# Mamba layer and gated FFN on one core: the dt products of two channel blocks in the upper and the lower rows of the array, with new order lists for the steady and the first chunk

## The chip, the core and the metric

The kernel runs on one core of a Trainium2 chip. That core has five engines that work side by side, each through its own list of instructions in order: TensorE (PE, matmuls, with its weight loads shown apart as PEld), VectorE (DVE), ScalarE (ACT), GpSimd (POOL) and SyncE (SP, which here only issues DMAs). They wait for one another through semaphores. The metric is the device time of one execution in microseconds. Before the change it is 1844.32 us, the median of 3 runs (1843.4 to 1846.78).

## The reference, cut to what matters

The input x is 8 rows of 1024 tokens of 256 channels, all float32. One layer is a Mamba block and a gated FFN, each with a residual and a LayerNorm. The part that the change touches is the step from `dbl` to `dt`.

```python
xz = einsum('bld,ed->ble', x, W_in); xi, z = split(xz, 2)           # 512 + 512 channels
u = silu(causal_conv4(xi, conv_w) + conv_b)
dbl = einsum('blc,ec->ble', u, W_xproj)                             # 16 + 16 + 16 columns
dt = softplus(einsum('blr,cr->blc', dbl[..., :16], W_dt) + b_dt)    # the dt products: K = 16
Bs, Cs = dbl[..., 16:32], dbl[..., 32:48];  A = -exp(A_log)         # 16 states
h = h * exp(dt_t * A) + (dt_t * u_t) * B_t;   y_t = sum_s h * C_t   # a scan over the tokens
y = (y + u * D_skip) * silu(z);  x1 = layernorm(x + y @ W_out.T)
out = layernorm(x1 + (silu(x1 @ wg.T) * (x1 @ wu.T)) @ wd.T)        # 768 hidden channels
```

## The kernel before

**Tiling.** The tokens are worked on in 16 chunks of 512, two for each of the 8 rows (`half` 0 and 1, the second going on from the state of the first). The 512 inner channels are 4 blocks (`cb`) of 128 partitions. A chunk has 64 scan steps, one for each block and state. A step is an `exp` on ACT (`decay_step`, into one of three PSUM banks), half a `drive` product on POOL (two states each, four buffers), and a scan on DVE (`scan`). Four steps make a quad, of which there are 16. PE transposes each quad's states (`transposes`, 4 groups g per quad), ACT copies each group to SBUF (`hT`, `evacuate`), and PE multiplies them with diagonals of C and sums over the states (`sum_states`, into the bank `yb`). Those products are 32 columns wide and the four of a group stand in the four column strips of the array.

**Stages.** Three chunks are in work at once. While the scans of chunk k run, the head of chunk k+1 (products `xi`, convolution, `u`, `xproj`, `dt`) and the tail of chunk k-1 (`out`, LayerNorm, `x1T`, `gate`, `up`, `down`) are put between them. All dense products share a ring of two PSUM banks in a fixed order (`products_in_order`, `room`), so each waits until the product two places before it is evacuated. The first chunk has no tail, and the last no head.

**Order.** Tables of numbers set which side item follows which scan step on each engine: a key (q, j) is a place after step j of quad q, and -1 is ahead of the quad's first. There are tables for steady chunks (`PE_SIDE`, `ACT_SIDE`, `DVE_SIDE`, `POOL_SIDE`), for the first (`..._FIRST`) and for the last (`..._LAST`). At the same place the engines are at different steps: ACT at step 4q+2+j, DVE at 4q+j, PE transposes the quad before, POOL makes drive 2q+j.

**The dt products.** `copy_dbl` (ACT) writes the 48 rows of `dbl`. `dt_proj` (PE) then multiplies the zero-padded `w_dt` (128 rows, of which 16 hold numbers) with `dbl` for each of the four blocks: a full-array product with 512 columns, which the profile shows as two MATMUL records. `add_bias` (ACT), `clamp` (DVE), `softplus_log` (ACT), `softplus_max` (DVE) and `dt_times_u` (POOL) follow. SP sends `dbl`'s B and C rows to DRAM and back, B spread over all partitions (`spread_bc`, `load_b`).

**POOL and the convolution.** `heads` on POOL prepares the first columns of `xi` for a later chunk and waits until all 12 taps of `conv` are done on DVE. All drives behind it wait with it.

**Setup.** Ahead of the first chunk each engine runs the head of chunk 0. There DVE makes `dtu` of block 0 alone (semaphore `f_dtu`), which is all that the first drives need; POOL makes that of block 1 itself in `drive_unit`.

## Time and profile before

| what | value |
|---|---|
| median of 3 runs | 1844.32 us |
| profiled execution: its own time | 1845.17 us |
| profiled execution: its span | 1843.2 us |
| PE busy | 1752.4 us (95%) |
| ACT busy | 1697.6 us (92%) |
| DVE busy | 1675.2 us (91%) |
| POOL busy | 1494.4 us (81%) |
| DMA queue q1, share of 16 engines | 18.3% |
| chain that ended last, by engine | PE 52%, ACT 25%, DVE 10%, issue 9%, POOL 3% |

The span is from the first to the last instruction, and 2.0 us of the execution's time lie around it. Busy shares are means over the whole span. What a stage is worth is read from a stretch of it. A PE busy time is a union of pipelined matmuls, whose ends are modelled.

### The profile page before, as it was taken

Reading aid. Unit: us, or ns where it says so; the run is one execution under the profiler, and the core shown is the slowest. Engines: PE = TensorE matmul, PEld = TensorE weight load, DVE = VectorE, ACT = ScalarE, POOL = GpSimd, SP = SyncE. Lnnn points to the kernel's source line nnn. Section 1 sums busy time; section 2 is a strip of 40 time slices with the busy share of each in tenths; the row PEclk is TensorE's granted clock in tenths of the full one; section 3 lists DMA queues with packets and bytes.
Section 4 is the critical chain, followed back from the end, with each engine's and each line's share of the span. In section 5 each row is a group of like instructions: output and inputs, shape, how many; then the busy total and the mean of one; then the engine's idle time right before and its main releaser. Section 6 shows DMA issues by size and latency. Waiting matters only on the chain.

```text
span 1843.2 us, 40373 instructions
## 1 busy us (share of the span) xinstructions
PE 1752.4 (95%) x15674; PEld 1213.6 (66%) x15674; DVE 1675.2 (91%) x1946; ACT 1697.6 (92%) x2927; POOL 1494.4 (81%) x847
## 2 busy tenths in 40 slices
PE   6679999999999999999999999999999999999997
PEld 2446676766667676676766667676676766667676
DVE  4999999999989999899989999999998999989984
ACT  5899999999999999999999999999999999999981
POOL 1997997879888787987879788787997879798950
PEclk9899999999999999999999999999999999999999
DMA  7030121301313120131301213130131311112000
GB/s 205 2 98 21 4 115 15 115 14 4 125 4 115 15 93 35 3 116 15 115 15 26 102 3 116 15 115 13 4 115 15 115 15 54 74 4 104 24 2 23
DMA packets 171342, 100.56 MB, mean 55 GB/s; under 512 B 139392, under 2 KB 157568, under 8 KB 162960
## 3 DMA queue, kind: packets, MB, share of 16 engines
q1 hardware_dynamic: 171152, 97.98, 18.3%
q8 instruction: 124, 2.03, 0.5%
q14 instruction: 66, 0.54, 0.1%
HBM read 88.52 MB, written 9.44 MB: 53 GB/s over the span
## 4 chain that ended last, share of the span: by engine, by line
PE 52%; ACT 25%; DVE 10%; issue 9%; POOL 3%; ACTq 0%; POOLq 0%; DVEq 0%
PE ring L1132 21%; PE tp L1111 15%; PE yb L1125 8%; ACT hT L684 7%; ACT decay L677 7%; DVE h L882 6%; PE ring L1220 4%; POOL drive L549 2%; ACT xi L695 1%; ACT sz L700 1%; ACT res L743 1%; ACT acc L693 1%; ACT u L710 1%; DVE acc L903 1%; ACT sz L714 1%
## 5 line engine op out<-in xcount | busy, mean ns | idle before, releaser
L549 POOL TENSOR_TENSOR drive<-dtu,b_all 128x1024 f32<-128x1024 f32 x512 | 1212.5, 2397 | 45.4 <-DVE h L882 41.2
L677 ACT ACTIVATE decay<-dt,a_neg 128x512 f32<-128x512 f32 x1024 | 702.7, 711 | 25.8 <-DVE h L882 24.7
L1111 PEld LDWEIGHTS tp<-ident,h 128*128 128x128 f32 x4096 | 462.0, 141 | 273.6 <-issue 153.1
L1111 PE MATMUL tp<-ident,h 128*128 128x128 f32 x4096 | 578.4, 278 | 64.8 <-ACT hT L684 47.9
L684 ACT ACTIVATE hT<-tp 128x512 f32<-128x512 f32 x1024 | 591.4, 606 | 46.8 <-PE tp L1111 44.9
L882 DVE TENSOR_TENSOR_SCAN h<-decay,h,drive 128x512 f32<-128x512 f32 x512 | 622.5, 1270 | 11.8 <-ACT decay L677 11.6
L882 DVE TENSOR_TENSOR_SCAN h<-decay,drive 128x512 f32<-128x512 f32 x512 | 592.9, 1210 | 23.1 <-ACT decay L677 21.3
L1125 PE MATMUL yb<-hT,diag_c 128*32 128x128 f32 x8192 | 273.9, 276 | 0.0
L1125 PEld LDWEIGHTS yb<-hT,diag_c 128*32 128x32 f32 x8192 | 209.9, 110 | 67.5 <-issue 44.4
L1132 PE MATMUL ring<-xt,w_in 128*128 128x512 f32 x512 | 238.3, 600 | 6.4 <-ACT xi L695 3.8
L903 DVE SCALAR_TENSOR_TENSOR acc<-xi,cw,acc 128x512 f32<-128x512 f32 x192 | 155.6, 830 | 29.4 <-ACT xi L695 25.4
L1132 PE MATMUL ring<-xt,w_u 128*128 128x512 f32 x360 | 169.5, 593 | 0.0
L1132 PE MATMUL ring<-xt,w_g 128*128 128x512 f32 x360 | 168.1, 596 | 0.0
L1132 PEld LDWEIGHTS ring<-xt,w_in 128*128 128x128 f32 x512 | 91.1, 192 | 88.9 <-issue 82.4
L568 POOL TENSOR_TENSOR spare_g<-eps,minus 128x4 f32<-128x4 f32 x17 | 4.1, 240 | 159.6 <-DVE acc L903 159.5
L579 POOL TENSOR_TENSOR dtu<-dt,u 128x1024 f32<-128x1024 f32 x31 | 74.1, 2390 | 58.3 <-DVE dt L917 58.3
L1220 PE MATMUL ring<-w_d,xi 128*128 128x256 f32 x480 | 113.5, 379 | 0.0
L1196 PE MATMUL ring<-w_out,yg 128*128 128x256 f32 x480 | 110.1, 382 | 0.1
L1132 PEld LDWEIGHTS ring<-xt,w_g 128*128 128x128 f32 x360 | 62.4, 190 | 59.8 <-issue 49.7
L1196 PEld LDWEIGHTS ring<-w_out,yg 128*128 128x128 f32 x480 | 88.8, 190 | 13.9 <-issue 3.1
L563 POOL TENSOR_TENSOR yg<-yg,sz 128x512 f32<-128x512 f32 x63 | 87.4, 1387 | 11.9 <-DVE yg L893 7.7
L1220 PEld LDWEIGHTS ring<-w_d,xi 128*128 128x128 f32 x480 | 88.9, 190 | 11.0 <-DVE hid L942 0.2
(128 smaller groups left out, 1612.2 us busy)
## 6 DMA issues: line engine op xcount, KB each, us to landing
...
c_col<-bc_scratch SPq DMA_DIRECT2D x256, 2.0 KB, 2.5
...
w_g<-in_w_gT SPq DMA_DIRECT2D x1, 768.0 KB, 7.1
w_u<-in_w_uT SPq DMA_DIRECT2D x1, 768.0 KB, 7.5
```

The costliest lines, as they stand in the source:

```text
L549: tt(drive[:, j % 4, :, :], src, b_all[:, n:n + 2, :], ALU.mult).then_inc(g_dr, 1)
L563: tt(yg[:, cb, :], yg[:, cb, :], sz[:, cb, :], ALU.mult).then_inc(g_y, 1)
L579: tt(dtu[:, two, :], dt[:, two, :], u[:, k.parity, two, :], ALU.mult).then_inc(g_dtu, 1)
L677: act(decay[decay_slot(k.parity, i)][:, :], dt[:, cb, :], ACT.Exp, scale=a_neg[:, cb, n:n + 1]).then_inc(a_da, 1)
L684: act(hT[:, (64 * k.index + g) % HTS, :], tp[g % 2][:, :], ACT.Copy).then_inc(a_ev, 1)
L882: nc.vector.tensor_tensor_scan(h[:, h_slot(k.parity, q), at:at + T, i % 4], decay[decay_slot(k.parity, i)][:, :], drive[:, (i // 2) % 4, i ...
L903: stt(acc[:, cb, :], xi[:, cb, tap:tap + T], cw[:, cb, tap:tap + 1], acc[:, cb, :], ALU.mult, ALU.add).then_inc(v_conv, 1)
L1111: last = nc.tensor.transpose(tp[g % 2][:, b * P:(b + 1) * P], h[:, h_slot(k.parity, q), t0:t0 + TS, :].rearrange("p t s -> p (t s)"), iden ...
L1125: last = mm(yb[b * TS:(b + 1) * TS, f * P:(f + 1) * P], diag_c[:, q % 4, 4 * f + b, :], hT[:, (64 * k.index + g) % HTS, b * P:(b + 1) * P] ...
L1132: last = mm(bank, lhsT, rhs, start=i == 0, stop=i == len(pairs) - 1)
L1196: last = mm(bank(k, "out", i)[:, half * DM:(half + 1) * DM], yg[:, c, tb * P:(tb + 1) * P], w_out[:, c, :], start=c == 0, stop=c == CB - 1)
L1220: last = mm(bank(k, "down", i)[:, half * DM:(half + 1) * DM], hidden_block(m)[:, tb * P:(tb + 1) * P], w_d[:, m, :], start=m == 0, stop=m ...
```

## The change

Three things are changed.

- `w_dt` gets a second copy of its 16 rows at partition 64, by one more DMA of the setup. In each chunk but the first SP also copies `dbl`'s 16 dt rows from partition 0 to partition 64, ahead of the copy to DRAM (semaphore `st_two`).
- For chunks 1 to 15 the dt products of two blocks are issued together as `dt_pair`: block cb from rows 0 to 63 of the array, block cb+1 from rows 64 to 127, into the two ring banks. Chunk 0 keeps the four single products.
- The eight tables of the steady and the first chunk are new. Those of the last chunk are as they were.

```diff
 PE_SIDE = {
-    (3, 3): [("xi", 2), ("xi", 3)], (4, 1): [("out", 0)], (4, 2): [("sum", 2), ("out", 1)],
-    (4, 3): [("xproj", 0)], (5, 2): [("sum", 3), ("dt", 0)], (5, 3): [("x1T", 0)],
+    (2, 3): [("sum", 0)], (3, 1): [("out", 0)], (3, 3): [("out", 1)], (4, 0): [("sum", 1)],
+    (4, 1): [("xproj", 0)], (4, 2): [("sum", 2)], (5, 0): [("dt", 0), ("dt", 1), ("sum", 3)],
...
 DVE_SIDE = {
-    (4, 1): [("max", 1), ("conv", 0, 1), ("conv", 1, 0), ("conv", 1, 1), ("conv", 2, 0), ("conv", 2, 1), ("conv", 3, 0), ("conv", 3, 1)],
+    (3, 3): [("conv", 0, 1), ("conv", 1, 0), ("conv", 1, 1), ("conv", 2, 0)],
+    (4, 0): [("conv", 2, 1), ("conv", 3, 0), ("r1", 0), ("conv", 3, 1)], (4, 1): [("r1", 1)],
...
 POOL_SIDE = {
-    (0, 1): [("std", 1)], (3, 0): [("diag", 1)], (4, 0): [("diag", 2), ("gate", 3)],
-    (4, 1): [("heads", 0), ("diag", 3)], (5, 1): [("std", 0)], (6, 1): [("dtu", 1)], (7, 1): [("gate", 0)],
+    (2, 0): [("diag", 1), ("diag", 2)], (2, 1): [("std", 1)], (3, 0): [("diag", 3)], (3, 1): [("gate", 3)],
+    (4, 0): [("heads", 0)], (5, 0): [("std", 0)], (6, 1): [("dtu", 1)], (13, 0): [("gate", 0)],
...
 DVE_FIRST = {
-    (0, -1): [("clamp", 1), ("conv", 0, 0), ("conv", 0, 1), ("conv", 1, 0), ("max", 1), ("conv", 1, 1), ("conv", 2, 0), ("conv", 2, 1)],
+    (0, -1): [("clamp", 1)], (1, 3): [("conv", 0, 0)], (2, 3): [("conv", 0, 1), ("max", 1), ("conv", 1, 0)],
...
 POOL_FIRST = {
-    (0, -1): [("dtu", 1)], (2, 1): [("first_diag", 0)], (3, 0): [("first_diag", 1), ("first_diag", 2)],
+    (2, 1): [("first_diag", 0), ("first_diag", 1), ("first_diag", 2)], (3, 1): [("dtu", 1)],
...
         loads = [
             (w_x[:, :, :], W_xT.rearrange("(a p) n -> p a n", p=P)),
             (w_dt[0:R, :], W_dtT),
+            (w_dt[P // 2:P // 2 + R, :], W_dtT),
...
             def spread_bc(k, with_b=False):
                 wait(eng, a_dbl, k.count(2, 2))
+                if k.index > 0:
+                    eng.dma_start(dbl[P // 2:P // 2 + R, :], dbl[0:R, :]).then_inc(st_two, 16)
                 eng.dma_start(bc_dram, dbl[R:R + 2 * N, :]).then_inc(st_bc, 16)
...
+            def dt_pair(k, cb):
+
+                if cb == 0:
+                    eng.wait_ge(st_two, 16 * k.index)
+                room(place["dt", cb, k.index])
+                room(place["dt", cb + 1, k.index])
+                for i in range(2):
+                    rows = slice(i * P // 2, (i + 1) * P // 2)
+                    product(bank(k, "dt", cb + i)[:, :], [(w_dt[rows, (cb + i) * P:(cb + i + 1) * P], dbl[rows, :])], p_dt)
+
...
+                elif what == "dt" and kind != "last":
+                    if of[0] % 2 == 0:
+                        dt_pair(k + 1, of[0])
                 elif in_chunk((what, *of), kind):
```

How this moves instructions is shown at three places. The first is PE in a steady chunk, from the x projection (`ring<-u,w_x`) on. `tp<-ident,h` are transposes, `yb` the sums over states, `ring<-dbl,w_dt` the dt products, `ring<-ident,res` and `ring<-ident,yt` transposes of x1 and y. Before:

```order
L1172 MATMUL ring<-u,w_x 48x256 x8
L1111 MATMUL tp<-ident,h 128x128 x12
L1125 MATMUL yb<-hT,diag_c 32x128 x16
L1132 MATMUL ring<-dbl,w_dt 128x512
L1111 MATMUL tp<-ident,h 128x128 x4
L1203 MATMUL ring<-ident,res 128x128 x4
L1111 MATMUL tp<-ident,h 128x128 x4
L1132 MATMUL ring<-dbl,w_dt 128x512
L1186 MATMUL ring<-ident,yt 128x128 x4
L1111 MATMUL tp<-ident,h 128x128 x4
```

And now, in the same place:

```order
L1177 MATMUL ring<-u,w_x 48x256 x8
L1116 MATMUL tp<-ident,h 128x128 x4
L1130 MATMUL yb<-hT,diag_c 32x128 x16
L1116 MATMUL tp<-ident,h 128x128 x8
L1137 MATMUL ring<-dbl,w_dt 128x512 x2
L1130 MATMUL yb<-hT,diag_c 32x128 x16
L1116 MATMUL tp<-ident,h 128x128 x8
L1218 MATMUL ring<-ident,res 128x128 x4
L1201 MATMUL ring<-ident,yt 128x128 x4
```

The pair stands behind the same work as the first single product did (three groups of transposes and one sum), but it now waits for `st_two` as well, and the next sum follows it directly.

The second place is DVE from the end of the setup into the first chunk; `dtu<-dt,u` is the last-but-one product of the setup, `acc<-xi` are taps of the convolution, `h<-decay,drive` are scans. Before:

```order
L1011 TENSOR_TENSOR dtu<-dt,u 128x512
L1008 TENSOR_TENSOR dt<-acc,dt 128x512
L911 TENSOR_SCALAR dt<-acc 128x1024
L903 SCALAR_TENSOR_TENSOR acc<-xi,cw,acc 128x512 x4
L917 TENSOR_TENSOR dt<-acc,dt 128x1024
L903 SCALAR_TENSOR_TENSOR acc<-xi,cw,acc 128x512 x5
L882 SCALAR_TENSOR_TENSOR h<-decay,drive 128x512 x32
```

And now:

```order
L1016 TENSOR_TENSOR dtu<-dt,u 128x512
L1013 TENSOR_TENSOR dt<-acc,dt 128x512
L916 TENSOR_SCALAR dt<-acc 128x1024
L887 SCALAR_TENSOR_TENSOR h<-decay,drive 128x512 x8
L908 SCALAR_TENSOR_TENSOR acc<-xi,cw,acc 128x512
L887 SCALAR_TENSOR_TENSOR h<-decay,drive 128x512 x4
L908 SCALAR_TENSOR_TENSOR acc<-xi,cw,acc 128x512 x2
L922 TENSOR_TENSOR dt<-acc,dt 128x1024
```

Nine taps and the maximum of blocks 2 and 3 stood ahead of the first scan; now one clamp stands there, and the taps are spread over the chunk.

The third place is POOL there; `drive<-dtu,b_all` are drives, `dtu<-dt,u 128x1024` the product for blocks 2 and 3, which waits for that maximum. Before:

```order
L649 MEMSET spare_f 128x1
L579 TENSOR_TENSOR dtu<-dt,u 128x1024
L549 TENSOR_TENSOR drive<-dtu,b_all 128x1024 x4
L543 TENSOR_TENSOR dtu<-dt,u 128x512
L549 TENSOR_TENSOR drive<-dtu,b_all 128x1024 x2
L557 TENSOR_TENSOR diag_c<-of_token,c_col 128x512
```

And now:

```order
L654 MEMSET spare_f 128x1
L554 TENSOR_TENSOR drive<-dtu,b_all 128x1024 x4
L548 TENSOR_TENSOR dtu<-dt,u 128x512
L554 TENSOR_TENSOR drive<-dtu,b_all 128x1024 x2
L562 TENSOR_TENSOR diag_c<-of_token,c_col 128x512 x3
L554 TENSOR_TENSOR drive<-dtu,b_all 128x1024 x2
L584 TENSOR_TENSOR dtu<-dt,u 128x1024
```

The product for blocks 2 and 3 no longer stands ahead of the first drive.

## Rows read from the trace of the kernel before

**Rows 1.** Timeline, DMA issues of one line: start us, us, what.
```profile
944.21 0.39 SPq L475 DMA_DIRECT2D out<-res  x1
...
1054.08 0.39 SPq L475 DMA_DIRECT2D out<-res  x1
```

**Rows 2.** Busy time by window, two neighbouring steady chunks, first scan to first scan.
```profile
369.34:479.38 110.04, 107.88 (x985) 74.62 (x978) 104.58 (x122) 105.88 (x184) 93.21 (x53) 1.00 0.19 55
479.38:589.30 109.92, 107.77 (x987) 74.64 (x982) 101.59 (x122) 105.63 (x184) 93.05 (x53) 1.00 0.19 55
```

**Rows 3.** Waits in 740 to 960 us (two chunks): us, times, longest.
```profile
ACT hT L684 <- PE tp L1111: 5.0, 9, 2.5
...
PE tp L1111 <- ACT hT L684: 4.1, 8, 0.8
```

**Rows 4.** Groups by line, one steady chunk (960 to 1070 us): busy us, mean ns.
```profile
L1132 PE MATMUL ring<-dbl,w_dt 128*128 128x512 f32 x8 | 4.3, 619 | 0.0
```

**Rows 5.** Timeline of PE in a steady chunk, a sum and two dt products.
```profile
961.43 1.08 PE L1125 MATMUL yb<-hT,diag_c 128*32 128x128 f32 x32
962.44 1.13 PE L1132 MATMUL ring<-dbl,w_dt 128*128 128x512 f32 x2
...
968.50 1.02 PE L1132 MATMUL ring<-dbl,w_dt 128*128 128x512 f32 x2
```

**Rows 6.** Line L1132 in 961 to 971 us, dt records: ns min/median/max.
```profile
L1132 PE MATMUL ring<-dbl,w_dt x6: 592/594/697, 962.4 to 968.9; 128*128 128x512 f32 x6
```

**Rows 7.** Timeline in the same chunk, ACT's copy of dbl and SP's issues.
```profile
959.39 0.77 ACT L720 ACTIVATE dbl<-ring 48x256 f32<-48x256 f32 x2
...
960.19 0.33 SPq L459 DMA_DIRECT2D bc_scratch<-dbl  x1
...
961.81 11.28 SPq L465 DMA_DIRECT2D c_col<-bc_scratch  x16
```

**Rows 8.** Timeline, setup and start of the first chunk, SP, POOL and DVE.
```profile
26.54 0.34 SPq L470 DMA_DIRECT2D b_all<-bc_scratch  x1
...
31.45 0.69 DVE L1011 TENSOR_TENSOR dtu<-dt,u 128x512 f32<-128x512 f32 x1
...
46.15 2.79 POOL L579 TENSOR_TENSOR dtu<-dt,u 128x1024 f32<-128x1024 f32 x1 [23.99 <-DVE dt L917]
48.90 11.04 POOL L549 TENSOR_TENSOR drive<-dtu,b_all 128x1024 f32<-128x1024 f32 x4
...
57.64 2.33 DVE L882 TENSOR_TENSOR_SCAN h<-decay,drive 128x512 f32<-128x512 f32 x2
...
148.28 1.27 DVE L882 TENSOR_TENSOR_SCAN h<-decay,h,drive 128x512 f32<-128x512 f32 x1
```

**Rows 9.** Tile b_all, 26 to 62 us: its loads' time to landing.
```profile
DMA to landing us min/median/max: 4.8/6.1/6.3
```

**Rows 10.** Busy time by window, end of the setup and first chunk.
```profile
33.00:148.30 115.30, 78.64 (x765) 51.19 (x766) 100.43 (x85) 100.28 (x168) 97.44 (x48) 0.88 0.27 72
...
57.60:148.30 90.70, 66.12 (x737) 46.04 (x738) 84.16 (x75) 83.44 (x145) 85.98 (x44) 0.88 0.22 60
```

**Rows 11.** Groups by line, 33 to 148.3 us: the convolution's taps.
```profile
L903 DVE SCALAR_TENSOR_TENSOR acc<-xi,cw,acc 128x512 f32<-128x512 f32 x12 | 18.7, 1563 | 7.1 <-ACT xi L695 6.9
```

**Rows 12.** Groups by line in 740 to 960 us, then timeline around heads.
```profile
L903 DVE SCALAR_TENSOR_TENSOR acc<-xi,cw,acc 128x512 f32<-128x512 f32 x24 | 18.1, 777 | 1.5 <-ACT xi L695 1.0
...
952.85 0.20 POOL L568 TENSOR_TENSOR spare_g<-eps,minus 128x4 f32<-128x4 f32 x1 [9.72 <-DVE acc L903]
...
954.05 4.70 POOL L549 TENSOR_TENSOR drive<-dtu,b_all 128x1024 f32<-128x1024 f32 x2
```

**Rows 13.** Setup: DMA issue, DVE's first use of the weights, landing time.
```profile
9.28 0.47 SPq L511 DMA_DIRECT2D w_d<-in_w_dT  x1
...
20.25 0.95 DVE L997 TENSOR_SCALAR w_g<-w_g 128x1536 f32<-128x1536 int32 x1
...
w_d<-in_w_dT SPq DMA_DIRECT2D x1, 768.0 KB, 9.2
```

More of the change, by code:

```diff
@@ L51 @@
 PE_SIDE = {
-    (0, 1): [("xi", 0), ("xi", 1)], (0, 3): [("z", 0), ("sum", 14)], (1, 0): [("sum", 15)], (1, 2): [("z", 1)],
-    (2, 0): [("z", 2), ("sum", 0)], (2, 1): [("turn", 3)], (3, 1): [("z", 3)], (3, 2): [("sum", 1)],
-    (3, 3): [("xi", 2), ("xi", 3)], (4, 1): [("out", 0)], (4, 2): [("sum", 2), ("out", 1)],
-    (4, 3): [("xproj", 0)], (5, 2): [("sum", 3), ("dt", 0)], (5, 3): [("x1T", 0)],
-    (6, 0): [("dt", 1), ("turn", 0)], (6, 1): [("sum", 4), ("x1T", 1), ("dt", 2), ("gate", 0)],
@@ L62 @@
-    (15, 0): [("down", 1)], (15, 3): [("sum", 13)],
+    (0, -1): [("xi", 0)], (0, 1): [("z", 0)], (0, 3): [("xi", 1), ("sum", 14), ("xi", 2)],
+    (1, 0): [("sum", 15), ("xi", 3), ("turn", 3)], (1, 2): [("z", 1)], (2, 0): [("z", 2)], (2, 2): [("z", 3)],
+    (2, 3): [("sum", 0)], (3, 1): [("out", 0)], (3, 3): [("out", 1)], (4, 0): [("sum", 1)],
+    (4, 1): [("xproj", 0)], (4, 2): [("sum", 2)], (5, 0): [("dt", 0), ("dt", 1), ("sum", 3)],
+    (5, 2): [("x1T", 0), ("turn", 0)], (5, 3): [("x1T", 1)], (6, 1): [("sum", 4), ("dt", 2), ("dt", 3)],
@@ new lines @@
+    (6, 3): [("gate", 0), ("up", 0)], (7, 1): [("gate", 1)], (7, 2): [("gate", 2)],
+    (8, 0): [("sum", 5), ("sum", 6)], (8, 2): [("up", 1), ("up", 2)], (8, 3): [("gate", 3)],
+    (9, 0): [("up", 3)], (9, 2): [("sum", 7), ("gate", 4)], (10, 0): [("gate", 5)], (10, 1): [("sum", 8)],
+    (10, 3): [("turn", 1)], (11, 1): [("sum", 9)], (11, 3): [("up", 4)], (12, 1): [("up", 5), ("sum", 10)],
+    (12, 3): [("down", 0)], (13, 1): [("sum", 11)], (13, 3): [("turn", 2)], (14, 1): [("sum", 12)],
+    (14, 3): [("down", 1)], (15, 3): [("sum", 13)],
@@ L92 @@
+    (5, 3): [("skip", 0)], (7, 0): [("gs", 0)], (7, 2): [("hid", 0)], (8, 2): [("gs", 1)], (8, 3): [("gs", 2)],
+    (9, 0): [("hid", 1)], (9, 1): [("hid", 2)], (10, 0): [("gs", 3)], (10, 1): [("clamp", 0)],
+    (10, 2): [("hid", 3)], (11, 1): [("gs", 4)], (11, 3): [("gs", 5)], (12, 1): [("skip", 1)],
+    (12, 3): [("hid", 4), ("hid", 5)], (13, 1): [("max", 0)], (14, 2): [("skip", 2), ("r2", 0)],
+    (15, 3): [("r2", 1)],
 }
 POOL_SIDE = {
-    (0, 1): [("std", 1)], (3, 0): [("diag", 1)], (4, 0): [("diag", 2), ("gate", 3)],
@@ L105 @@
+    (3, 2): [("sum", 1), ("xi", 3), ("z", 2)], (4, 1): [("sum", 2)], (5, 1): [("z", 3), ("sum", 3)],
+    (6, 1): [("xproj", 0)], (6, 3): [("sum", 4)], (7, 2): [("sum", 5)], (8, 0): [("dt", 0), ("dt", 1)],
+    (8, 1): [("sum", 6)], (8, 3): [("turn", 0)], (9, 0): [("sum", 7)], (9, 3): [("dt", 2), ("dt", 3)],
+    (10, 3): [("sum", 8)], (11, 3): [("turn", 1), ("sum", 9)], (13, 1): [("sum", 10), ("sum", 11), ("turn", 2)],
+    (14, 0): [("sum", 12)], (15, 0): [("sum", 13)],
 }
 ACT_FIRST = {
[16 rows of a table removed]
[17 rows of a table added]
 }
 DVE_FIRST = {
-    (0, -1): [("clamp", 1), ("conv", 0, 0), ("conv", 0, 1), ("conv", 1, 0), ("max", 1), ("conv", 1, 1), ("conv", 2, 0), ("conv", 2, 1)],
@@ L133 @@
-    (5, 0): [("first_diag", 3)], (8, 1): [("heads", 0)], (15, 0): [("gate", 0)],
-    (15, 1): [("gate", 1), ("dtu", 0), ("gate", 2), ("diag", 0)],
+    (2, 1): [("first_diag", 0), ("first_diag", 1), ("first_diag", 2)], (3, 1): [("dtu", 1)],
+    (4, 0): [("first_diag", 3)], (6, 1): [("heads", 0)], (12, 0): [("gate", 0)],
+    (14, 1): [("gate", 1), ("dtu", 0)], (15, 1): [("gate", 2), ("diag", 0)],
 }
@@ L401, in mamba_ffn @@
         l_in = [sem("l_in0"), sem("l_in1")]; l_cv = sem("l_cv"); l_w = sem("l_w"); l_xt = [sem("l_xt0"), sem("l_xt1")]; l_res = sem("l_res")
-        st_bc = sem("st_bc"); l_c = [sem(f"l_c{g}") for g in range(4)]; l_b = [sem(f"l_b{g}") for g in range(4)]
+        st_bc = sem("st_bc"); st_two = sem("st_two"); l_c = [sem(f"l_c{g}") for g in range(4)]; l_b = [sem(f"l_b{g}") for g in range(4)]
         st_out = sem("st_out")
```

27 lines of the change are left out of this document (7 added, 20 removed), and 69 rows, old and new, of tables (ACT_FIRST, ACT_SIDE).

## Prediction

> **What bounds the kernel now.** I read the timeline of SP's stores first, since one falls in each chunk: they come 109.87 us apart [rows 1], so 14 steady chunks make some 1540 of the 1845.2 us of the profiled execution. The busy times by window then say who fills such a chunk [rows 2]. PE is busy 107.9 of 110.0 us, ACT 105.9, DVE 101.6 to 104.6, POOL 93.2, and PE's granted clock is 1.00 (the level of 2.4 GHz), so there is no clock to win. PE has 2.1 us left per chunk, ACT 4.2. The waits [rows 3] tell what PE's rest is: per two chunks PE waits 4.1 us for ACT's copies of the transposes, and ACT 5.0 us for PE's transposes. They stop each other a little at a time. So PE's work sets the steady chunk, and ACT's would set it 4 us lower.
>
> The first chunk is another case. The first scan starts at 57.64 us and the first scan of the next chunk at 148.28 [rows 8]. From the end of the setup (33 us) to there, 115.3 us, DVE is busy 100.4, ACT 100.3, POOL 97.4 and PE 78.6 us [rows 10]. No engine is full, because the scans start late. POOL's first drive stands behind a dtu product for which it sat idle for 23.99 us, and DVE's first scan behind nine taps [rows 8].
>
> **The change in the steady chunk.** Four dt products, eight records, take PE 4.3 us per chunk [rows 4]. A single one takes 1.02 to 1.13 us [rows 5]. Now there are two pairs. If the halves of a pair run side by side, a pair costs as much as one product at the dear end, 1.13 us. What speaks for it is the sum over states: 16 products, in the four column strips, take 1.08 us together, and a dt product has four times their columns and takes 1.02 us [rows 5], so one after another the 16 would take about 16 x 0.25 = 4 us. That is with strips of columns; halves of rows do not occur in this trace. So two pairs cost 2.26 us and 4.3 - 2.26 = 2.04 us go. The bounds for a pair are 1.0 us (the cheaper product) and 2.15 us (no overlap, half of 4.3), a gain of 2.3 to 0 per chunk; I take the value nearest to the sum's row.
>
> The pair changes the way in which the array is divided. The first dt record behind a sum takes 697 ns against a median of 594 [rows 6], 0.10 us for a changed division. Each pair adds about one such edge, so 0.2 us per chunk come off: 1.84 us of PE's work go. The Trainium skill, "TensorEngine Tiling (Array Packing)", Key Properties, says that a change of tiling mode drains the engine; the 697 ns agree, and by that rule alone the sum would be the same.
>
> The pair waits for a new DMA. In the trace ACT's copy of dbl ends at 960.16, SP issues at 960.19, and the next instruction that waits for that landing starts at 961.81 [rows 7]: 1.62 us. The copy of dbl's rows now stands first in that queue, so it lands about 1.65 us after ACT's copy. PE in between has, from the order, one group of transposes, a sum and two more groups behind the x projection, about as much as was ahead of the first dt product, which started 2.28 us after ACT's copy (962.44) [rows 5]. But the pair now stands directly behind the group of transposes that waits for the hT copied right behind dbl, where before a sum stood, at 961.43 [rows 5]: 1.27 us after ACT's copy. So a stall of 0.4 us, between 0 and 0.7 us. Behind it on PE wait a sum and transposes, and ACT's hT copies for those. The second DMA, to DRAM, is issued 0.33 us later; its users (the diagonals and drives of the next chunk) come tens of us later, so I put that at nothing, and at 0.3 us per chunk if the cover were gone.
>
> PE's work falls to 107.9 - 1.84 = 106.0 us, next to ACT's 105.8. With 0.4 us for the stall the chunk would be 110.0 - 1.44 = 108.6 us if PE's rest stays 2.1 us. Two engines that are equally full meet more often, but the new lists are also free to place the work anew; from the order I can't price that, so I let both stand against each other: between plus 1.4 us (nothing gained) and minus 1.0 (no stall, and a part of the rest gone). ACT's, DVE's and POOL's work is unchanged in number. That gives 14 x 1.44 = 20 us; at the ends 14 x 2.4 = 34 and 0.
>
> **The change in the first chunk.** DVE now has only a clamp (done by 35 us) and POOL nothing ahead. The first drive needs the dtu of block 0, done at 31.45 + 0.69 = 32.1, and the first block of B, issued at 26.54 and landing after 4.8 to 6.3 us [rows 8, 9], so at 32.8 at the latest. It can start 48.9 - 32.9 = 16 us earlier. That is the upper bound of the gain. The work that stood there is not gone but spread over the chunk: DVE has 100.4 us of it, and idled 90.7 - 84.2 = 6.5 us in the scanning part [rows 10]. Starting at 34.3 it arrives at 34.3 + 100.4 + 6.5 = 141.2 instead of 148.3: 7 us. ACT, by its 100.3 us and 90.7 - 83.4 = 7.3 us idle, arrives at 33 + 107.6 = 140.6; POOL earlier. The taps weigh 1563 ns each here and 777 ns in a steady chunk [rows 11, 12], the slow ones being those beside POOL's drives; if half of that excess of 12 x 0.79 = 9.4 us goes, 5 us more are won. I take 9 us, between 0 (PE or ACT stops the scans instead; PE has 78.6 us of work and room for it) and 14.
>
> **The setup.** One more load stands ahead of the weights, 0.5 us in SP's queue. The last load would land at 9.28 + 0.5 + 9.2 = 19.0, and DVE first uses such a weight at 20.25, with no wait ahead [rows 13]. Nothing, then; 0.5 us if that cover is gone.
>
> **The sum.** 20 + 9 = 29 us off the profiled execution's 1845.2 us gives 1816. The median of the runs shown lies 0.9 us below that execution, so the forecast is 1815 us. The last chunk's lists are as before and it has no head, so it gives nothing.
>
> **The rivals.**
> (B) The halves do not overlap, or half. A product is two records. If all matmuls started strictly in the order A1, A2, B1, B2, and a half's second record waited for its first, a pair would take three steps of the four: 1.13 x 1.5 = 1.7 us, a gain of 4.3 - 3.4 - 0.2 - 0.4 = 0.3 us per chunk, 4 us in all; with the first chunk 13, so 1831; with no overlap at all 1835 or a little more. Against it: the sum's 16 products have the same two records each (32 in the row), and by that rule would need at least 17 steps of about 0.11 us, 1.9 us, where the trace has 1.08 [rows 5]. The Trainium skill, "TensorE: Matmul & The Clock Gate", Part 3, The mechanism, has matmuls start and end in program order with no reordering, from which this rival follows; the row speaks against it here unless the records are issued in turn.
> (C) The steady chunk stays at 110 us: PE becomes shorter, but its rest grows by as much, since it and ACT now wait for each other more (they do 9 and 8 times per two chunks [rows 3]). Then only the first chunk's 9 us remain: 1835. For it: ACT is at 96%. Against it: ACT still has 4.2 us per chunk.
> (D) Slower. In a steady chunk the convolution now stands three quarters of a quad earlier on DVE (behind step 15, before behind step 17), and `heads` behind drive 8 instead of drive 9. POOL idles 9.72 us at `heads` [rows 12], and with one drive fewer in store DVE's scans behind the convolution find POOL one drive late. A drive is 2.35 us (half of 4.70), and if the last of them still runs beside the first taps, two of these are slowed by 0.79 us each [rows 11, 12]. With none of it hidden that is 3.9 us per chunk against 1.44 gained: (3.9 - 1.44) x 14 - 9 = 25 us slower, 1869. It turns slower from 1.44 + 9 / 14 = 2.1 us per chunk unhidden. Against it: DVE has 5 to 8 us of rest per chunk [rows 2], and a rearrangement of r1 behind the taps covers one drive (2 us).
>
> **How the numbers follow.** Forecast 0.65, B 0.08, C 0.16, D 0.11. A measurement of this kernel can tell about 0.2% (3.7 us) from no change. Faster: the forecast, B, and C but for a part in which the first chunk gives nothing either: 0.65 + 0.08 + 0.11 = 0.84. Same 0.04. Slower: D and a little of C, 0.12. The forecast's own range is 1797 (34 + 14 us) to 1829 (half of the forecast's gain); taking in B and C's main case the range is 1797 to 1840, which leaves out D and the tails.
>
> **What the changed profile would show.** The dt line of a steady chunk at about 2.3 us busy; 3.4 would be B. PE busy near 106 us of a period near 108.6. The first scan at about 36 us in place of 57.64, the first scan of the second chunk near 139. The wait of the pair for the new copy near 0.4 us; over 1 us would make my price of the DMA wrong. A period of 110 with the dt line halved is C; waits of scans for drives behind the convolution are D.

## The result, and the profile after

| | median | range of the runs | profiled span |
|---|---|---|---|
| before | 1845.8 us | 1843.4 to 1847.6 | 1843.2 us |
| after | 1848.7 us | 1846.0 to 1852.3 | 1844.6 us |

The ratio after to before is 1.0018, with a 95% interval of 1.0011 to 1.0024. The forecast was 1815 us, with a range of 1797 to 1840. So there is no gain, and rather a small loss. The profiled execution of the kernel after took 1846.35 us, which is near the fastest of its 20 runs and 2.4 us under their median, so the traces show a little less of the loss than the medians do.

The first half of the forecast came true. The timeline of DVE and POOL at the start of the changed kernel (start us, us, what), which answers to [rows 8]:

```profile
31.54 9.79 POOL L554 TENSOR_TENSOR drive<-dtu,b_all 128x1024 f32<-128x1024 f32 x4 [9.87 <-DMA b_all<-bc_scratch]
...
32.47 1.96 DVE L916 TENSOR_SCALAR dt<-acc 128x1024 f32<-128x1024 f32 x1 [1.53 <-ACT acc L730]
...
34.35 2.33 DVE L887 TENSOR_TENSOR_SCAN h<-decay,drive 128x512 f32<-128x512 f32 x2
...
137.33 1.27 DVE L887 TENSOR_TENSOR_SCAN h<-decay,h,drive 128x512 f32<-128x512 f32 x1
```

The first scan starts at 34.35 instead of 57.64 us and the second chunk at 137.33 instead of 148.28: 10.95 us are won there. But the last chunk starts at 1689.62 us where it started at 1688.90. So the 14 steady chunks gave back 11.7 us, the first of them 0.7, and what follows the start of the last chunk takes another 0.75 us, which together makes the 1.4 us between the two profiled spans. The busy times by window for two neighbouring steady chunks (length, then busy us of PE, PEld, DVE, ACT and POOL, the clock, the DMA share, GB/s) answer to [rows 2]:

```profile
470.86:581.28 110.42, 107.21 (x988) 74.00 (x980) 101.53 (x121) 106.16 (x184) 92.76 (x53) 1.00 0.20 55
581.28:692.59 111.31, 107.38 (x984) 73.90 (x980) 105.00 (x122) 106.00 (x184) 92.95 (x53) 1.00 0.19 54
```

The period is 110.4 and 111.3 us in turn, where it was 109.9 and 110.0. The forecast was 108.6. PE is busy only 0.5 us less than before, though its dt products became 2 us shorter. The groups by line of PE in the second of these windows (busy us, mean ns | idle before), of which the dt line answers to [rows 4]:

```profile
L1137 PE MATMUL ring<-xt,w_in 128*128 128x512 f32 x32 | 15.5, 606 | 0.0
...
L1137 PE MATMUL ring<-xt,w_g 128*128 128x512 f32 x24 | 11.6, 604 | 0.0
...
L1137 PE MATMUL ring<-dbl,w_dt 64*128 64x512 f32 x8 | 2.3, 641 | 0.6 <-DMA dbl<-dbl 0.6
```

The dt line is at the 2.3 us that were forecast. The same 32 and 24 records of `w_in` and `w_g` took 14.7 and 11.2 us in a chunk before. Their count, form and clock are the same, and 1.2 us of "busy" have come back in them. The `w_in` line also takes 15.5 us in c_single (below), which has the new lists and no pair, so that part comes with the lists. The page warns that the ends of matmuls are modelled, so a small change of PE's busy time is no clean measure of its work.

The chain that ended last has changed hands. Its shares by engine, from the page of the kernel after:

```profile
PE 35%; DVE 25%; issue 15%; ACT 15%; POOL 9%; ACTq 0%; POOLq 0%; DVEq 0%
```

Before, they were PE 52%, ACT 25%, DVE 10%, issue 9%, POOL 3%.

### The profile page after: what moved, and what is told of

The parts are those of the page before. It is cut to its first block, busy times and chain, and to the rows that moved or that the text cites. A ratio compares the mean times of both kernels' runs of the same rounds, so it can differ in the third digit from the quotient of the medians.

```text
span 1844.6 us, 40402 instructions
## 1 busy us (share of the span) xinstructions
PE 1739.7 (94%) x15674; PEld 1201.4 (65%) x15674; DVE 1675.3 (91%) x1946; ACT 1699.5 (92%) x2925; POOL 1490.5 (81%) x847
## 4 chain that ended last, share of the span: by engine, by line
PE 35%; DVE 25%; issue 15%; ACT 15%; POOL 9%; ACTq 0%; POOLq 0%; DVEq 0%
DVE h L887 16%; PE ring L1137 12%; PE tp L1116 10%; POOL drive L554 6%; PE yb L1130 6%; ACT decay L682 5%; ACT hT L689 5%; PE ring L1235 4%; DVE acc L908 4%; DVE xi L942 1%; DVE xi L947 1%; ACT yt L710 1%; POOL rstd L593 1%; PE decay L1347 1%; ACT acc L730 1%
## 5 line engine op out<-in xcount | busy, mean ns | idle before, releaser
L689 ACT ACTIVATE hT<-tp 128x512 f32<-128x512 f32 x1024 | 584.1, 606 | 31.8 <-PE tp L1116 31.0
L1137 PE MATMUL ring<-xt,w_in 128*128 128x512 f32 x512 | 247.9, 608 | 4.8 <-ACT acc L730 2.6
L1137 PE MATMUL ring<-xt,w_g 128*128 128x512 f32 x360 | 172.7, 602 | 0.0
L908 DVE SCALAR_TENSOR_TENSOR acc<-xi,cw,acc 128x512 f32<-128x512 f32 x192 | 144.0, 770 | 13.8 <-ACT xi L700 10.8
L1211 PE MATMUL ring<-w_out,yg 128*128 128x256 f32 x480 | 108.6, 379 | 0.1
L562 POOL TENSOR_TENSOR diag_c<-of_token,c_col 128x512 f32<-128x512 f32 x64 | 71.2, 1114 | 43.5 <-PE yb L1130 43.5
L1137 PEld LDWEIGHTS ring<-xt,w_u 128*128 128x128 f32 x360 | 62.4, 190 | 58.9 <-issue 44.9
```

What stands on the lines that cost most here:

```text
L562: tt(diag_c[:, g, :, :], mask, col, ALU.mult).then_inc(g_dc, 1)
L689: act(hT[:, (64 * k.index + g) % HTS, :], tp[g % 2][:, :], ACT.Copy).then_inc(a_ev, 1)
L908: stt(acc[:, cb, :], xi[:, cb, tap:tap + T], cw[:, cb, tap:tap + 1], acc[:, cb, :], ALU.mult, ALU.add).then_inc(v_conv, 1)
L1137: last = mm(bank, lhsT, rhs, start=i == 0, stop=i == len(pairs) - 1)
L1211: last = mm(bank(k, "out", i)[:, half * DM:(half + 1) * DM], yg[:, c, tb * P:(tb + 1) * P], w_out[:, c, :], start=c == 0, stop=c == CB - 1)
```

## What the stages of one chunk say

The forecast rested on busy shares over a whole chunk. Here is the same steady chunk cut into three stages, first of the kernel before (the columns as above):

```profile
589.30:629.30 40.00, 38.72 (x345) 26.06 (x335) 37.94 (x48) 39.91 (x70) 29.58 (x20) 1.00 0.04 15
629.30:669.30 40.00, 39.38 (x349) 24.72 (x350) 36.95 (x37) 39.51 (x71) 38.07 (x22) 1.00 0.13 4
669.30:699.30 30.00, 29.75 (x292) 23.80 (x294) 29.63 (x38) 26.45 (x45) 25.56 (x14) 1.00 0.46 176
```

And of the kernel after:

```profile
581.28:621.28 40.00, 39.19 (x352) 26.17 (x344) 37.64 (x48) 39.39 (x69) 25.33 (x20) 1.00 0.04 15
621.28:661.28 40.00, 37.45 (x318) 22.93 (x320) 36.21 (x36) 38.94 (x70) 38.00 (x19) 1.00 0.13 4
661.28:692.59 31.31, 30.74 (x324) 24.80 (x320) 31.16 (x40) 27.67 (x48) 29.62 (x16) 1.00 0.46 169
```

Before, ACT is full in the first stage (39.91 of 40). In the last one PE and DVE are full together (29.75 and 29.63 of 30). The 4.2 us that the forecast left to ACT lie nearly all in the last stage (3.55 us), where ACT could not use them. In the middle stage, in which the dt products lie, PE is at 39.38 of 40, but ACT is at 39.51 and POOL at 38.07 beside it. After, PE does fall there, to 37.45. ACT stays at 38.94, and the last stage has DVE at 31.16 of 31.31.

The chain of waits over the middle stage says whose work ends last. Before, its shares by line:

```profile
by line: PE ring L1132 49.6%; PE tp L1111 27.8%; PE yb L1125 15.2%; PE ring L1203 3.0%; issue 1.7%; ACT hT L684 1.5%; PE ring L1186 1.3%; ACT dbl L720 1.1%
```

After:

```profile
by line: DVE h L887 40.0%; issue 18.8%; ACT hT L689 9.7%; ACT decay L682 8.8%; DVE xi L942 6.5%; DVE xi L947 5.0%; ACT res L748 4.1%; ACT xt L742 2.9%; ACT acc L730 2.5%; DVE dt L916 1.7%; ACT yt L710 1.5%; ACT dbl L725 0.9%; DVEq L946 0.1%
```

PE was on 97% of that chain and is now on none of it. This reading seems to support the forecast (as if PE bounded the middle stage), and yet nothing was won. A chain names one path among several that are nearly as long, and says nothing of the next one. Only cuts tell that, and they are the second group of experiments.

## The experiments

Unless another edit stands there, "before" and "after" are the two kernels. Periods are those of neighbouring steady chunks, in us. The kernel before had a median of 1843.7 to 1846.7 us on the chips of the four groups, and each ratio is against it on the same chip.

| run | edit | median us | ratio (95%) | periods |
|---|---|---|---|---|
| a_first | before, new first-chunk lists | 1834.9 | 0.9952 (0.9940 to 0.9964) | 109.95 / 110.07 |
| c_single | after, single dt products, no copies | 1849.7 | 1.0031 (1.0020 to 1.0042) | 110.57 / 111.35 |
| b_pair | before, pairs in the old lists | 1932.1 | 1.0469 (1.0456 to 1.0483) | 113.9 to 119.1 |
| e_both | b_pair with new first-chunk lists | 1925.9 | 1.0454 (1.0431 to 1.0478) | 113.9 to 119.1 |
| b_moved | before, b_pair's lists, single products | 1912.5 | 1.0362 (1.0347 to 1.0378) | 113.9 to 115.6 |
| q_before | before, dt products halved | 1843.0 | 0.9982 (0.9972 to 0.9991) | 109.86 / 109.94 |
| p_before | before, 4 of 6 up products halved | 1839.1 | 0.9968 (0.9955 to 0.9981) | 109.62 / 109.72 |
| n_before | before, DVE's gs cut to a quarter | 1842.4 | 0.9982 (0.9972 to 0.9991) | 109.97 |
| n_after | after, the same cut | 1846.7 | 1.0003 (0.9993 to 1.0012) | 110.49 / 110.94 |
| c_before | before, 8 of ACT's silus halved | 1840.6 | 0.9965 (0.9951 to 0.9979) | 109.62 / 109.65 |
| pn_before | p and n together | 1833.4 | 0.9938 (0.9923 to 0.9952) | 109.32 |
| pnc_before | p, n and c together | 1825.2 | 0.9894 (0.9878 to 0.9911) | 108.82 |
| g_act_copy | after, second copy made by ACT | 1858.0 | 1.0067 (1.0052 to 1.0082) | 111.2 / 112.1 |
| v_xi | after, ACT's xi 0 one step later | 1856.4 | 1.0061 (1.0044 to 1.0078) | 111.0 / 111.9 |
| v_heads | after, `heads` behind drive 9 | 1872.0 | 1.0144 (1.0128 to 1.0159) | 112.3 / 113.1 |
| v_diag | after, diagonal 2 later | 1847.5 | 1.0012 (1.0003 to 1.0022) | 110.4 / 111.3 |

### The change taken apart

a_first puts the four new lists of the first chunk (`PE_FIRST`, `ACT_FIRST`, `DVE_FIRST` and `POOL_FIRST`) into the kernel before and nothing else:

```diff
 DVE_FIRST = {
-    (0, -1): [("clamp", 1), ("conv", 0, 0), ("conv", 0, 1), ("conv", 1, 0), ("max", 1), ("conv", 1, 1), ("conv", 2, 0), ("conv", 2, 1)],
...
+    (0, -1): [("clamp", 1)], (1, 3): [("conv", 0, 0)], (2, 3): [("conv", 0, 1), ("max", 1), ("conv", 1, 0)],
```

> The kernel before with the four first-chunk lists of the changed kernel alone; steady lists, single dt products and copies are those of before. In the changed trace the second chunk's first scan came at 137.3 us instead of 148.3. If the first chunk is worth that by itself, this run is 9 to 11 us faster than before (ratio 0.995 to 0.994) with steady periods of 109.9 and 110.0. If the late start was only hiding work that the next chunk has to make up, its second period grows and the gain is under 4 us.

Measured: 1834.9 us, 0.5% (8.8 us) under before and 0.7% under after; its profiled span is 10.9 us under that of before. The second chunk starts at 137.26 us, as in the kernel after (137.33). Its steady chunks have the periods of before:

```profile
577.82:687.91 110.09, 107.94 (x987) 74.63 (x980) 104.57 (x122) 105.97 (x184) 93.25 (x53) 1.00 0.19 55
687.91:797.86 109.95, 107.80 (x987) 74.63 (x980) 101.58 (x122) 105.66 (x184) 93.07 (x53) 1.00 0.19 55
```

So the first chunk's term is shown, and this is the version to keep: it beats both kernels.

c_single is the kernel after with its new lists, but with single products and without the two copies:

```diff
-                if k.index > 0:
-                    eng.dma_start(dbl[P // 2:P // 2 + R, :], dbl[0:R, :]).then_inc(st_two, 16)
...
-                elif what == "dt" and kind != "last":
-                    if of[0] % 2 == 0:
-                        dt_pair(k + 1, of[0])
```

> The changed kernel's eight new lists with single dt products and without the copies. Theory 1, the lists have moved the bound to DVE's waits: the pair hardly matters in them, so the period stays near 110.9 on average and the time within 6 us of the changed kernel. Rival, the pair or its copy is at fault: this run is 5 us or more faster than the changed kernel. If PE bounds in the new lists too, this run is 15 to 25 us slower.

Measured: 1849.7 us, within the error of the kernel after (1.0020 to 1.0042 against 1.0011 to 1.0024), with the same periods to 0.15 us, and a dt line of 3.9 us. (Two neighbouring chunks of its profiled execution, of 113.70 and 109.68 us, fall out of the row; why is open.) Two things follow. The new steady lists by themselves cost 15 us by the medians against a_first, which differs only by them; the 14 steady chunks of the two traces make it 14.3, of which 1.4 lie in the two odd chunks. And within these lists the pairs save 1.6 us of PE's dt line and 0.04 to 0.15 us of the period. The new lists are made for pairs: in c_single, too, two dt products stand together. What lists free of that demand would cost is not measured.

b_pair puts the pairs into the old lists, with the second of each pair moved up to the first and the bias of block 3 beside that of block 2; e_both adds the new first-chunk lists. The edit of `PE_SIDE`:

```diff
-    (4, 3): [("xproj", 0)], (5, 2): [("sum", 3), ("dt", 0)], (5, 3): [("x1T", 0)],
-    (6, 0): [("dt", 1), ("turn", 0)], (6, 1): [("sum", 4), ("x1T", 1), ("dt", 2), ("gate", 0)],
+    (4, 3): [("xproj", 0)], (5, 2): [("sum", 3), ("dt", 0), ("dt", 1)], (5, 3): [("x1T", 0)],
+    (6, 0): [("turn", 0)], (6, 1): [("sum", 4), ("x1T", 1), ("dt", 2), ("dt", 3), ("gate", 0)],
```

> The pair and its copy of dbl alone, in the lists of before: dt 1 is moved up to dt 0, dt 3 to dt 2, with the bias of block 3 beside that of block 2, nothing else. Theory 1, the new steady lists are at fault and the pair is good: steady period 108.5 to 109.3 and 10 to 20 us faster than before. Rival, a shorter PE gives nothing here since ACT or DVE holds the period (C): period 109.8 to 110.1 and within 3 us of before. Second rival, the copy and its wait are at fault: PE waits over 1 us per chunk for the copy and the run is 5 to 15 us slower.

> The steady lists of before with the pair put in as in b_pair, and the new first-chunk lists. If the two parts add, its gain is that of a_first plus that of b_pair: 20 to 31 us faster than before by theory 1, 9 to 11 us if the pair gives nothing. This would beat both kernels.

b_pair was 88 us slower than before, where the worst case expected was 15, and e_both 82 us slower, where a gain of 9 us or more was expected. b_moved asks whether the pair does it or the place: b_pair's lists, single products.

> The lists of b_pair with single dt products and no copy: only dt 1, dt 3 and the biases are moved. If b_pair's 88 us came from two dt products standing together in a ring of two banks, so that both products behind them wait for ACT's biases, this run is as slow, 70 to 100 us slower than before. If the copy and its wait or the row halves did it, this run is within 15 us of before.

It took 1912.5 us. The order alone costs 66 us, a little under the 70 to 100 that were expected if it was at fault, and b_pair lies another 20 us higher. The timeline of PE in b_moved shows the first two dt products back to back and what comes then:

```profile
649.75 1.98 PE L1132 MATMUL ring<-dbl,w_dt 128*128 128x512 f32 x4
651.57 0.60 PE L1111 MATMUL tp<-ident,h 128*128 128x128 f32 x4
652.26 0.66 PE L1203 MATMUL ring<-ident,res 128*128 128x128 f32 x4
652.76 0.60 PE L1111 MATMUL tp<-ident,h 128*128 128x128 f32 x4
655.28 0.66 PE L1186 MATMUL ring<-ident,yt 128*128 128x128 f32 x4 [1.93 <-ACT acc L725]
```

Two dt products together hold both banks of the ring, and what follows on PE waits 1.93 us until ACT has read one. This is what the pair costs besides its products: it needs two banks at one time, so it can't be had without new lists.

The other 20 us are not work of the pair or its copy. The clock column of the windows shows it, first a chunk of b_moved, then two of b_pair:

```profile
721.86:835.77 113.91, 108.27 (x990) 74.79 (x982) 101.61 (x121) 106.07 (x184) 93.24 (x53) 1.00 0.18 53
```

```profile
726.90:840.78 113.88, 106.86 (x990) 74.13 (x983) 101.65 (x121) 106.03 (x184) 93.17 (x53) 1.00 0.18 53
958.00:1076.98 118.98, 112.16 (x991) 76.87 (x984) 101.64 (x122) 106.12 (x184) 93.22 (x53) 0.94 0.18 51
```

At full clock a chunk takes 113.9 us with and without the pair, 4 us more than before. The longer chunks are those in which PE's granted clock falls to half (the level of 1.2 GHz) for a while, first at or just after the wait of 1.9 us; from 1006.0 to 1019.7 us of b_pair, for example, it is 0.50. In b_moved that holds for 31 us of the 14 steady chunks in sum, in b_pair for 99 us, in the kernel before for 3.4 and in the kernel after for none. So of the 88 us of b_pair some 56 are the 4 us per chunk, and most of the rest is lost clock. Whether the clock falls more often because the pair leaves PE less work at this place was not tested.

### Cuts: what an engine's work is worth

Each cut leaves out a part of the columns of one kind of instruction in the kernel before, without moving any. First the dt products, whose shortening was the change's aim:

```diff
-                product(bank(k, "dt", cb)[:, :], [(w_dt[:, cb * P:(cb + 1) * P], dbl[:, :])], p_dt)
+                product(bank(k, "dt", cb)[:, 0:T // 2], [(w_dt[:, cb * P:(cb + 1) * P], dbl[:, 0:T // 2])], p_dt)
```

> The kernel before with its dt products over 256 of the 512 columns (the other half of dt's input is left out, so its values are stale). It takes about 2 us of work off PE per chunk, as the pair does, and moves no instruction, changes no evacuation and adds no copy. If PE's work bounds the steady chunk, the period falls from 110.0 to 108.0 to 108.7 and the run is 18 to 28 us faster. If ACT and DVE hold the period as well, it stays above 109.3 and the gain is under 10 us.

The dt line in one chunk, and the window of that chunk:

```profile
L1132 PE MATMUL ring<-dbl,w_dt 128*128 128x256 f32 x8 | 2.6, 406 | 0.0
```

```profile
587.22:697.17 109.95, 106.55 (x984) 74.47 (x979) 104.55 (x122) 105.81 (x184) 93.33 (x53) 1.00 0.19 55
```

PE's dt line is 1.7 us shorter and the period falls by 0.06 us, to 109.9. (The run is 3.3 us shorter by its ratio, but not by this: in its trace the second chunk starts at 145.06 us instead of 148.28, that first steady chunk is 1.35 us longer than before, and the 13 behind it give 0.8 us together.) This is the test of the forecast's main step. It needs no pair, no copy and no new list, and the step fails it.

The same for other work: p_before halves the up products of blocks 2 to 5, n_before and n_after cut DVE's `gs` to a quarter of the columns, c_before halves eight of ACT's silus.

```diff
+                cols = T // 2 if weight is w_u and m >= 2 else T
+                product(to[:, 0:cols], [(weight[:, d, m * P:(m + 1) * P], x1[:, d, 0:cols])
...
+                stt(hidden_block(m)[:, 0:T // 4], hidden_block(m)[:, 0:T // 4], 1.0, bank(k, "gate", m)[:, 0:T // 4], ALU.add, ALU.mult).then_inc(v_gs, 1)
...
+                act(sz[:, cb, 0:T // 2], sz[:, cb, 0:T // 2], ACT.Silu).then_inc(a_sz, 1)
```

> The kernel before with the DVE operation gs over 128 of 512 columns (three quarters of the gate product left out), about 0.4 us shorter each, six per chunk: 2.4 us less DVE work per chunk. If PE bounds the lists of before, under 6 us faster (period 109.6 or more). If DVE bounds them too, 20 us or more.

> The changed kernel with the same DVE operation over 128 of 512 columns: 2.4 us less DVE work per chunk, all of it behind quad 6. If the new lists have moved the bound to DVE (its work plus its waits), the period falls by 1.5 to 2.4 us from 110.9, some 20 to 30 us less than the changed kernel. If PE or ACT still bounds them, under 8 us less.

> The kernel before with the up products of blocks 2 to 5 over 256 of 512 columns (the other half left out): about 1.8 us less PE work per chunk, in quads 8 to 12, where PE stands without a gap. If PE alone sets that stage, the period falls by 1.3 to 1.8 us (18 to 25 us). If DVE is tied with PE there (both without a gap), under 6 us, as when DVE's gs was shortened.

> The kernel before with the silu of u (from chunk 2 on) and of z over half of their columns (the other half is left without it): some 0.24 us less on ACT for each of eight operations, 1.9 us per chunk, seven of them at quad 4. The chain of waits runs over ACT in the first 40 us of a steady chunk. If ACT sets that stage, the period falls by 1.2 to 1.9 us from 110.0, 17 to 27 us in all. If the bound is PE over the whole chunk, or the three engines are tied there, under 5 us.

> The cuts of p_before and n_before together: 1.8 us of PE's and 2.4 us of DVE's work less per chunk, both in quads 7 to 13. If the two engines are tied in this stage, together they bring what neither does alone: a period 1.0 to 1.8 us lower, 14 to 25 us in all. If the gains only add, under 8 us.

> The cuts of p_before, n_before and c_before together (half of four up products, three quarters of gs, half of the silus left out): about 1.8 us less on PE, 2.4 on DVE, 1.9 on ACT per chunk. If the chunk is tied between these three, so that each stage passes from one to the next, the period falls by 1.5 to 2.5 us (21 to 35 us in all), well above the sum of the single gains. If they only add, it falls by 0.7 to 1.1 us. If a chain of handovers that none of the cuts shortens holds it, it also stays at 109 or more.

In p_before each product is added up from two parts, so the cut was 3.4 us (the line `w_u` went from 11.3 to 7.9 us) and not the 1.8 expected. Per chunk, in the order of the table: 1.7 us off PE give 0.06 us, 3.4 us off PE 0.3, 2.4 us off DVE nothing (n_before's 0.18% do not show in the steady chunks of its trace), 1.7 us off ACT 0.3, PE and DVE together (5.8) 0.65, and all three together (7.5) 1.15. The window of a chunk of the last:

```profile
580.14:688.95 108.81, 105.55 (x985) 74.42 (x977) 102.39 (x121) 103.92 (x184) 93.23 (x53) 1.00 0.19 55
```

No work that was cut sets the steady chunk by itself, and the three cuts together convert at 15%. In the forecast 1.84 us converted in full. Singly, p_before and c_before gained 5.9 and 6.5 us in all, near the under 6 and under 5 that were expected of a tie. The joint gains are about twice the sum of the single ones, as engines tied with one another would give. But pn_before (11 us in all) and pnc_before (20 us, 1.15 per chunk) stayed under what was expected of a tie (14 to 25, and 21 to 35 us) and above what was expected if the gains only add. So a tie of the three explains a part; what holds the remaining 108.8 us is open. POOL (93 of 110 us, and 38.07 of 40 in the middle stage) was never cut, and neither it nor a chain of handovers between engines is ruled out. n_after in the changed kernel gives 0.15 us on average, though the chain of the kernel after runs over DVE: the chain's engine is not a bound there either.

### Work added, and items of the new lists moved

g_act_copy takes the pair's DMA away: ACT writes the second copy from the same bank.

```diff
-                    eng.dma_start(dbl[P // 2:P // 2 + R, :], dbl[0:R, :]).then_inc(st_two, 16)
...
+                    for b in range(2):
+                        act(dbl[P // 2:P // 2 + R, b * T // 2:(b + 1) * T // 2], bank(k, "xproj", 0)[b * P // 2:b * P // 2 + R, 0:T // 2],
+                            ACT.Copy).then_inc(st_two, 1)
```

> The changed kernel with the second copy of dbl's dt rows written by ACT (two more operations of some 0.37 us behind the copy of dbl) in place of SP's DMA. The pair's wait for the copy (0.6 us of PE) goes and ACT gets 0.75 us more. If that wait costs time, 5 to 9 us less than the changed kernel; if ACT's work is what counts at this place, 3 to 12 us more.

PE's wait for the copy is gone, and the period is longer by 0.8 us. The groups by line show what came in its place, two ACT copies at the start of the middle stage, where ACT is at 38.94 of 40 in the kernel after:

```profile
L1139 PE MATMUL ring<-dbl,w_dt 64*128 64x512 f32 x8 | 2.3, 641 | 0.0
...
L727 ACT ACTIVATE dbl<-ring 16x256 f32<-16x256 f32 x2 | 0.7, 374 | 0.0
```

So 0.75 us added to ACT at this place count in full. PE's stall was moved and not taken away: the copies hold up ACT's hT copy behind them, and PE now waits 1.65 us for that ahead of the pair, where it waited 0.84 for it and 0.61 for the DMA:

```profile
626.00 0.63 PE L1118 MATMUL tp<-ident,h 128*128 128x128 f32 x4 [1.65 <-ACT hT L687]
626.55 1.13 PE L1139 MATMUL ring<-dbl,w_dt 64*128 64x512 f32 x4
```

v_heads tests rival D: it moves `heads` back behind drive 9, where the old lists had it, so that POOL has one drive more in store.

```diff
-    (4, 0): [("heads", 0)], (5, 0): [("std", 0)], (6, 1): [("dtu", 1)], (13, 0): [("gate", 0)],
+    (4, 1): [("heads", 0)], (5, 0): [("std", 0)], (6, 1): [("dtu", 1)], (13, 0): [("gate", 0)],
```

> The changed kernel with POOL's heads moved from (4, 0) to (4, 1), behind drive 9, as it stood before. In the changed kernel DVE waits 1.4 us per chunk for a drive behind the convolution. If rival D is what makes the new lists slow, 10 to 20 us less than the changed kernel. If the wait is hidden elsewhere, or the drive beside the taps slows them by as much, within 4 us of it.

It became slower by some 1.8 us per chunk. The timeline of the kernel after has the six first taps together at 4.42 us:

```profile
605.14 4.42 DVE L908 SCALAR_TENSOR_TENSOR acc<-xi,cw,acc 128x512 f32<-128x512 f32 x6
```

In v_heads they take 6.18 us, because the first of them now runs beside a drive:

```profile
609.08 4.72 POOL L554 TENSOR_TENSOR drive<-dtu,b_all 128x1024 f32<-128x1024 f32 x2
...
611.86 6.18 DVE L908 SCALAR_TENSOR_TENSOR acc<-xi,cw,acc 128x512 f32<-128x512 f32 x6
```

The 1.76 us more are about the growth of the period, and DVE's wait for a drive is gone. The new place of `heads` is thus the better of the two for these lists, the reverse of what rival D held against it.

v_diag moves the third diagonal from (2, 0) to (3, 0) of `POOL_SIDE`, v_xi ACT's copy of the first xi block from (0, 1) to (0, 2) of `ACT_SIDE`.

> The changed kernel with POOL's diagonal 2 moved from (2, 0) to (3, 0). It waits there 3.1 us for PE's sum 14, and with it all drives behind it. If this wait is what makes the new lists slow, 5 to 15 us less than the changed kernel. If POOL's lead of four drives covers it, within 3 us.

> The changed kernel with one item moved on ACT: the copies of xi 0 from (0, 1) to (0, 2), behind the decay of step 4, for which DVE waits 1.44 us at the start of a steady chunk. If DVE's chain bounds the chunk, up to 1.4 us per chunk come back: 10 to 20 us less than the changed kernel. If it is just one wait of many and another takes its place, within 5 us of it.

v_diag changed nothing that the steady periods show, as expected if POOL's lead covers the wait. v_xi made them 0.6 us longer and the run 8 us slower than the kernel after, which neither of its two cases had. None of the three items, moved alone, brings back any of the 15 us.

## Why the prediction was wrong

**The failed step is "So PE's work sets the steady chunk".** From it followed that 1.84 us less of PE's work would be 1.84 us less of the period (1.44 with the stall), and 20 of the 29 us. q_before shows what this kind of work is worth: 1.7 us off the very same products give 0.06 us per chunk. The 107.9 of 110 us were a mean over three stages: ACT full in the first, PE with ACT and POOL at its heels in the second, PE and DVE in the third. The rows of [rows 3], in which PE and ACT wait for each other about equally, were read as friction at the edge of PE's bound. They fit a tie better. The Trainium skill, "Perfetto Trace Analysis", Identifying the Most-Contended Engine, says that matmul busy time is no good measure of TensorE's headroom and that the share of the weight loads, beside the rate of useful arithmetic, should be taken. Here that speaks against the forecast, and the runs agree: the weight loads filled 74.6 of 110 us [rows 2]. Its next advice, to optimize the engine with the highest occupancy first, would lead to ACT, and c_before shows only 0.33 us for 1.7 us there.

**The new steady lists cost more than the pair can give.** The forecast said that their placing could not be priced from the order and put it between minus 1.0 and plus 1.4 us per chunk around its value, so at worst nothing gained. In fact a_first against c_single makes it 15 us, some 0.6 us in one chunk and 1.3 in the next, where the forecast allowed no loss. That end of the range was wrong: an order written anew can be worse than the old one.

In the longer of two neighbouring chunks, the first loss that stays is in the sixth of the 16 quads (q = 5). Up to its start the two kernels are level: it begins 39.8 us into the chunk before and 39.9 after. The timeline of DVE there, before:

```profile
629.06 4.78 DVE L882 TENSOR_TENSOR_SCAN h<-decay,h,drive 128x512 f32<-128x512 f32 x4
636.68 0.75 DVE L893 SCALAR_TENSOR_TENSOR yg<-u,dsk,ring 128x512 f32<-128x512 f32 x1 [2.83 <-PE ring L1186]
637.34 3.63 DVE L882 TENSOR_TENSOR_SCAN h<-decay,h,drive 128x512 f32<-128x512 f32 x3
```

And after (the quad's first scan is the second of the three at 620.00):

```profile
620.00 3.61 DVE L887 TENSOR_TENSOR_SCAN h<-decay,h,drive 128x512 f32<-128x512 f32 x3
624.99 1.28 DVE L887 TENSOR_TENSOR_SCAN h<-decay,h,drive 128x512 f32<-128x512 f32 x1 [1.38 <-POOL drive L554]
626.87 1.28 DVE L887 TENSOR_TENSOR_SCAN h<-decay,h,drive 128x512 f32<-128x512 f32 x1 [0.59 <-ACT decay L682]
628.74 0.75 DVE L898 SCALAR_TENSOR_TENSOR yg<-u,dsk,ring 128x512 f32<-128x512 f32 x1 [0.59 <-PE ring L1201]
630.49 2.46 DVE L887 TENSOR_TENSOR_SCAN h<-decay,h,drive 128x512 f32<-128x512 f32 x2 [1.01 <-ACT decay L682]
```

Before, DVE had its four scans at once and then one wait of 2.83 us; after, it waits four times, first for a drive, and the next quad starts 48.0 us into the chunk before and 49.2 after. The quad takes as long in c_single (39.9 and 49.2), so the pair and its copy are not the cause. In the shorter of the two chunks the same loss appears (48.1 and 49.0 us) but is made up by the twelfth quad, which starts at 77.3 and 77.4 us, and the 0.5 us of its period are lost behind that. Of the waits over two chunks (us, times, longest) these have grown, after:

```profile
DVE h L887 <- ACT decay L682: 8.7, 14, 1.5
...
DVE h L887 <- POOL drive L554: 2.9, 2, 1.5
...
PE ring L1137 <- DMA dbl<-dbl: 1.2, 2, 0.6
```

Before, there were 3.5 us for the decays and no wait for a drive. Against that, DVE's wait for PE's transposes of y fell from 6.3 to 1.8 us, so the grown waits are not the loss by themselves. That the waits cause the longer period is a reading of the trace, not a test: which entries of the four new lists cost the 15 us stays open, and the three that were moved here are not it.

**What was right.** The first chunk: forecast 9 us, and 10.95 in the trace; a_first has it alone (8.8 us by the medians). The taps in it fell from 1563 to 1166 ns each, 4.8 us together, where the forecast put 5. The 16 us that it called the upper bound were no bound: the first scan came 23.3 us earlier, since its own taps had held it longer than the drive did. PE's granted clock in this chunk was 0.88 before [rows 10] and 0.93 after; what that gave is not known. The overlap of the halves: a pair takes 1.13 us and the line 2.3, where rival B had 3.4. The copy: SP issues it at 621.54 and the pair starts at 623.52 with a stall of 0.61 us, within the 0 to 0.7 forecast. The timeline of PE and SP in the kernel after, which answers to [rows 5, 7]:

```profile
622.28 0.63 PE L1116 MATMUL tp<-ident,h 128*128 128x128 f32 x4 [0.84 <-ACT hT L689]
623.52 1.13 PE L1137 MATMUL ring<-dbl,w_dt 64*128 64x512 f32 x4 [0.61 <-DMA dbl<-dbl]
624.58 1.08 PE L1130 MATMUL yb<-hT,diag_c 128*32 128x128 f32 x32
```

```profile
621.54 0.57 SPq L463 DMA_DIRECT2D dbl<-dbl  x1
622.16 0.58 SPq L464 DMA_DIRECT2D bc_scratch<-dbl  x1
```

**The rivals.** C (the steady chunk stays) came nearest, and its sign, a period of 110 with the dt line halved, is nearly what is seen. PE's rest did grow, from 2.1 to between 3.2 and 3.9 us, but C allowed no loss; its 1835 us are what a_first measures. D had the wait for the drive right in kind (1.4 us, priced at up to 2.35) and wrong in its cause: with `heads` back in its old place (v_heads) the kernel is slower still. The loss is of D's sign but from the lists as a whole. The ledger, in per cent of the time before: minus 0.48 by the first-chunk lists (a_first), plus 0.79 by the new steady lists (c_single against a_first), minus 0.13 by the pairs (after against c_single, not resolved, since the intervals overlap), in sum plus 0.18, or 3.3 us.
